# Four neighbouring engines' orders changed together: values before keys, token variance before the score bias, tokens before the second turn, squares summed by rows before gate 0

## The reference

```python
x = x + attention(ln_c(x))     # ln_c: over the 64 channels; 8x8 windows, 4 heads of 16, softmax(q k + bias) v, projection
t = tokens(x)                  # 16384 tokens of 64 channels per image
t = t + moe(ln_t(t))           # router: softmax of 8 logits, top 2, shares renormalised; 8 experts, 64x64 each, with bias
x = back(t)
```

## Time and profile before

| | |
|---|---|
| time, median of 3 runs | 1269.74 us (1269.69 to 1274.37) |
| the profiled execution | 1268.81 us, span 1267.0 us |
| busy: PE, DVE, ACT, POOL | 1192.4, 1053.9, 920.4, 1081.7 us |
| granted clock of PE over the span | 0.983 of full speed |
| the chain that ended last | PE 67%, DVE 10%, POOL 7%, DMA 7%, issue 5%, ACT 5% |

### The profile page before, as it was taken

One profiled execution on the slowest core, in us unless ns is written; L12 is line 12 of the kernel. 1 busy time (PEld: TensorE's weight loads), 2 busy tenths in 40 slices (PEclk: granted clock), 3 DMA queues, 4 the chain that ended last, 5 costly groups with the idle time before them and its releaser, 6 DMA issues.

```text
span 1267.0 us, 47630 instructions
## 1 busy us (share of the span) xinstructions
PE 1192.4 (94%) x19840; PEld 729.4 (58%) x19840; DVE 1053.9 (83%) x2247; ACT 920.4 (73%) x1743; POOL 1081.7 (85%) x925
## 2 busy tenths in 40 slices
PE   4579999999999999999999999999999999999986
PEld 3456666655565666656566666655556565666531
DVE  6458898888888889898888888988888888888874
ACT  6368778867777887877677888777767776777742
POOL 6368999989888999999988899998988888888753
PEclk9599999999999999999999999999999999999998
DMA  7012333322223233322222333332222222222221
GB/s 203 5 38 66 92 94 86 81 61 71 55 60 81 77 90 94 91 59 61 70 55 62 95 88 86 88 87 55 58 65 66 53 65 65 63 56 66 64 70 42
DMA packets 95622, 91.43 MB, mean 72 GB/s; under 512 B 26928, under 2 KB 62384, under 8 KB 95408
## 3 DMA queue, kind: packets, MB, share of 16 engines
q1 hardware_dynamic: 95408, 88.37, 27.6%
HBM read 35.90 MB, written 17.83 MB: 42 GB/s over the span
## 4 chain that ended last, share of the span: by engine, by line
PE 67%; DVE 10%; POOL 7%; DMA 7%; issue 5%; ACT 5%; SPq 0%; DVEq 0%; POOLq 0%; ACTq 0%
PE bank_y L530 16%; PE bank_s L410 8%; PE bank_t L425 8%; PE bank_s L384 6%; PE bank_o L464 4%; PE bank_g L518 4%; DMA r_b<-recip_rows 4%; PE bank_o L438 4%; PE bank_p L454 4%; PE bank_p L518 3%; DVE t_g L992 3%; DMA recip_rows<-r_out 2%; PE bank_t L394 2%; PE bank_y L502 2%; DVE prob L880 2%
## 5 line engine op out<-in xcount | busy, mean ns | idle before, releaser
L1142 POOL TENSOR_TENSOR t_g<-t_t,g_copy 128x512 f32<-128x512 f32 x192 | 245.6, 1292 | 72.0 <-ACT g_copy L712 70.8
L530 PE MATMUL bank_y<-t_g,w_exp 128*64 128x512 f32 x1024 | 268.9, 616 | 6.7 <-DVE t_g L992 4.7
L1120 POOL TENSOR_TENSOR prob<-prob,mx 128x512 f32<-128x512 f32 x256 | 261.8, 1045 | 14.7 <-DVE mx L887 14.5
L675 ACT ACTIVATE prob<-prob 128x512 f32<-128x512 f32 x256 | 159.4, 623 | 128.6 <-POOL prob L1120 128.6
L992 DVE TENSOR_TENSOR t_g<-t_t,bank_p 128x512 f32<-128x512 f32 x256 | 174.2, 680 | 9.2 <-PE bank_p L518 7.3
L880 DVE TENSOR_TENSOR prob<-bank_s,rel 128x1024 f32<-128x1024 f32 x128 | 156.3, 1221 | 28.4 <-PE bank_s L410 23.7
L425 PE MATMUL bank_t<-idn,prob 128*128 128x128 f32 x1024 | 163.6, 283 | 5.5 <-ACT v_bd L670 5.0
L679 ACT ACTIVATE prob_t<-bank_t 128x512 f32<-128x512 f32 x256 | 152.5, 596 | 21.3 <-PE bank_t L425 21.2
L712 ACT ACTIVATE g_copy<-bank_g 128x512 f32<-128x512 f32 x192 | 113.8, 593 | 74.1 <-PE bank_g L518 73.9
L425 PEld LDWEIGHTS bank_t<-idn,prob 128*128 128x128 f32 x1024 | 112.8, 141 | 79.2 <-issue 65.9
L887 DVE TENSOR_REDUCE mx<-prob 128x16 f32<-128x1024 f32 x128 | 155.4, 1214 | 2.2
(11 more groups left out here) (122 smaller groups left out, 2345.1 us busy)
## 6 DMA issues: line engine op xcount, KB each, us to landing
t_t<-t_rout SPq DMA_DIRECT2D x256, 128.0 KB, 2.4
x_in<-in_x SPq DMA_DIRECT2D x68, 256.0 KB, 3.3
r_b<-recip_rows SPq DMA_DIRECT2D x64, 256.0 KB
out_y<-y_out SPq DMA_DIRECT2D x128, 128.0 KB, 2.6
r_in<-sum_b SPq DMA_DIRECT2D x64, 16.0 KB
recip_rows<-r_out SPq DMA_DIRECT2D x64, 16.0 KB, 1.7
t_g<-in_sel SPq DMA_DIRECT2D x1, 512.0 KB, 3.6
rel<-in_relb SPq DMA_DIRECT2D x1, 256.0 KB, 2.9
```

Of the source, the lines that this page charges most:

```text
L530: mm(B_Y[C * a:C * a + C, :], w_exp[:, pair, :], t_g[:, (2 * pair + a) % TG, :], start=False, stop=(pair == MIXES // 2 - 1), skip_group_ch ...
L675: A(prob[:, i], prob[:, i], ACT.Exp).then_inc(p_ready.sem, 1)
L1120: G.tensor_tensor(sc, sc, mx[:, i, :].unsqueeze(2).broadcast_to([P, 2 * HEADS, NTOK]), ALU.subtract).then_inc(s_shifted.sem, 1)
L1142: G.tensor_tensor(t_g[:, u % TG, :], t_t[:, p, u % 2, :], g_copy[:, n, :], ALU.mult).then_inc(tg_pool.sem, 1)
```

## The change

PE's `values` stands before the key and value projection, and `turn_tokens` before the second turn. On ACT the turned gates and the tokens are copied between the two key copies, and the values after the second turn's copy in every slot; in take slots the second block is copied out before the first one is squared. On DVE `token_variance` stands before `bias`, `reciprocals` before `total_squares`, and `sum_squares` before gates 0 and 1. The squares are written as [128 rows, 8], so that ACT writes 32 bytes apart and DVE reads 8 neighbours. No operation is added or removed.

```diff
--- before.py
+++ after.py
@@ -110,7 +110,7 @@
 
         x_in = sb("x_in", [P, RING, 4, W])
-        x_sq = sb("x_sq", [P, 2, 4, H])
+        x_sq = sb("x_sq", [P, H, 2 * 4])
...
@@ -152,7 +152,7 @@
...
-        FIRST_SQ = (x_sq, prob[:, 0:2].rearrange("p i h n k -> p (i h n k)").rearrange("p (m c h) -> p m c h", m=2, c=4))
+        FIRST_SQ = (x_sq, prob[:, 0:2].rearrange("p i h n k -> p (i h n k)").rearrange("p (h x) -> p h x", x=2 * 4))
         B_S = ctx.enter_context(nc.psum_tensor("bank_s", [P, 2, BANK], F32))
         B_T, B_O, B_E, B_P, B_G, B_Y = (
             ctx.enter_context(nc.psum_tensor(f"bank_{n}", [P, BANK], F32)) for n in "toepgy")
@@ -540,19 +540,19 @@
                     prob_sums(j - 1, 1 - p)
                 if attending:
                     turn_probs(j, 0, work)
+                if outputting:
+                    values(j - 1, 1 - p)
                 if projecting:
                     project(j + 1, KEYS_VALUES)
-                if outputting:
-                    values(j - 1, 1 - p)
                 if mixing:
                     residual(j - 3, 1 - p)
                     turn_gates(j - 3)
+                if routing_on:
+                    turn_tokens(j - 2)
                 if work.take:
                     take(work.batch, *work.take, 0, j)
                 elif attending:
                     turn_probs(j, 1, work)
-                if routing_on:
-                    turn_tokens(j - 2)
                 if mixing:
                     expert_biases(j - 3)
                     gates(j - 3, 0)
@@ -625,7 +625,8 @@
                 act.wait_ge(xt_ready.sem, xt_ready.at(n, 2 * r + m + 1))
                 act.wait_ge(sq_sums.sem, sq_sums.at(batch, max(t * 2 + r - (batch == 0), 0)))
                 act.sem_inc(passed, 1)
-                A(dst[:, m], xt[:, bass.ds(plane + (2 * r + m) * 4, 4), :], ACT.Square).then_inc(sq_ready.sem, 1)
+                A(dst[:, :, 4 * m:4 * m + 4].rearrange("p h c -> p c h"), xt[:, bass.ds(plane + (2 * r + m) * 4, 4), :],
+                  ACT.Square).then_inc(sq_ready.sem, 1)
 
             def first_take(batch, t, r):
                 for m in range(2):
@@ -726,19 +727,18 @@
                     copy_result(j - 4)
                 if projecting:
                     copy_k(j + 1, 1 - p, 0)
+                if mixing:
+                    copy_turned_gates(j - 3)
+                if routing_on:
+                    copy_tokens(j - 2)
+                if projecting:
                     copy_k(j + 1, 1 - p, 1)
-                    if not work.take:
-                        copy_v(j + 1)
-                if mixing:
-                    copy_turned_gates(j - 3)
                 if work.take:
                     take(work.batch, *work.take, 0, B_T[:, :])
-                if routing_on:
-                    copy_tokens(j - 2)
-                if projecting and work.take:
+                elif attending:
+                    copy_probs(j, p, 1)
+                if projecting:
                     copy_v(j + 1)
-                if attending and not work.take:
-                    copy_probs(j, p, 1)
                 if routing_on:
                     copy_logits(j - 2)
                 if attending and work.take:
@@ -757,8 +757,8 @@
                 if routing_on:
                     gate_exp(j - 2)
                 if work.take:
+                    take(work.batch, *work.take, 1, B_T[:, :])
                     square_planes(work.batch, *work.take, 0)
-                    take(work.batch, *work.take, 1, B_T[:, :])
                 if mixing:
                     copy_gates(j - 3, 6)
                 if attending:
@@ -817,7 +817,7 @@
                 pair = bass.ds(t * 2 + r, 1)
                 dve.wait_ge(sq_ready.sem, sq_ready.at(n, 2 * r + 2))
                 V.tensor_reduce(sums2[:, :, pair].rearrange("p h o -> p (h o)"),
-                                src[:, :, :, :].rearrange("p m c h -> p h (m c)"), AX.X,
+                                src[:, :, :], AX.X,
                                 ALU.add).then_inc(sq_sums.sem, 1)
 
             def first_sums(batch, t, r):
@@ -995,27 +995,27 @@
                 projecting, attending, outputting, routing_on, mixing = stages(on)
                 if mixing:
                     routing(j - 3, 9, 14)
+                if routing_on:
+                    token_variance(j - 2)
                 if attending:
                     bias(j, 1)
-                if routing_on:
-                    token_variance(j - 2)
                 if mixing:
                     routing(j - 3, 15, 19)
                 if attending:
                     maxima(j, 1)
+                if outputting:
+                    reciprocals(j - 1)
                 if work.step == SQUARES:
                     total_squares(work.batch)
-                if outputting:
-                    reciprocals(j - 1)
                 if work.step == PLANES:
                     total_planes(work.batch)
                 if work.step == SCALES:
                     turn_root(work.batch)
+                if work.sums:
+                    sum_squares(work.batch, *work.sums)
                 if mixing:
                     gate(j - 3, 1 - p, 0)
                     gate(j - 3, 1 - p, 1)
-                if work.sums:
-                    sum_squares(work.batch, *work.sums)
                 if routing_on:
                     routing(j - 2, 1, 8)
                 if mixing:
```

More of the change, by code:

```diff
@@ L728, in slot @@
                     copy_k(j + 1, 1 - p, 0)
-                    copy_k(j + 1, 1 - p, 1)
-                    if not work.take:
-                        copy_v(j + 1)
                 if mixing:
                     copy_turned_gates(j - 3)
+                if routing_on:
+                    copy_tokens(j - 2)
+                if projecting:
+                    copy_k(j + 1, 1 - p, 1)
                 if work.take:
                     take(work.batch, *work.take, 0, B_T[:, :])
-                if routing_on:
-                    copy_tokens(j - 2)
-                if projecting and work.take:
+                elif attending:
+                    copy_probs(j, p, 1)
+                if projecting:
                     copy_v(j + 1)
-                if attending and not work.take:
-                    copy_probs(j, p, 1)
                 if routing_on:
```

## The result

The changed kernel takes **1301.85 us** (median of 4 runs, 1300.98 to 1302.6), the kernel before 1269.97 us beside it; the ratio is 1.0236, 95% interval 1.0219 to 1.0254. The change costs 31.9 us.

A forecast was written before the change was run, and what follows sets the result against it. PE, busy 18.58 of 18.70 us in a steady group, was taken as the bound. Take slots +7.7, plain +10.4, sum -0.7, statistics +3.3 and filling +1 made about +22: 1291 us, eight-in-ten range 1280 to 1303.

The forecast's parts named there:

- The copies behind the later keys: ACT, seven copies from first key to l_t: l_t complete 0.62 us later, PE's gates 3 +0.51 plain, +0.42 take.
- Plain slots: 24 slots without input turns, sums or statistics: 14 grow by 0.51 us and 10 by 0.33, +10.4 in all.
- the late DMA chain: Reciprocals and their two DMAs start 0.3 us later; about ten plain slots, where PE waits behind them, grow by 0.33.
- Values in front cover the bias: PE's projection start: moved to t = 3.66 with 0.3 us of cover from values; without them it would stall 0.7.
- Take slots j%16 = 7 to 10: Among 24 slots that also turn two input blocks: each 0.42 us longer less 0.10 from the shorter reduce, +7.7 in all.
- Statistics slots: Nine slots (j%16 = 12 to 14) doing a statistics step: +0.3, +0.3 and +0.5 us, three times, +3.3.
- the rival of the stalled projection: If ACT's square ends after t = 1.8 in most slots, everything slides 0.3 us in 57 slots: 1308 us, chance 0.07.
- The squares by rows: DVE's reduce 0.77 us shorter in 28 slots; ACT's square 0 to +0.38 longer; start 0 to +3, taken as 0.
- Sum slots: Three slots that only sum squares (j%16 = 11): from 18.71 to 18.46 us, -0.7 in all, turn_logits covering gate 0.

## Why the prediction was right, and where its sizes were off

The forecast of 1291 in 1280 to 1303, slower with 0.86, held: 1301.85, at the upper end. The mechanism was right and the parts together were a third too low; the terms that were mis-sized are named below.

- **The copies behind the later keys (right).** L_t was put at t = 8.35 to 8.72 and came at 8.30 to 8.70. In between, first key 4.83 (forecast 4.83), g_t 5.62 (5.61), t_rout 6.11 (6.11), second key 6.59 (6.61). Gates 3 was to start at 8.87 and does at 8.91. Plain slots 18.48, forecast 18.45. The experiment with l_t ahead of the second probabilities shows the cause: with l_t 0.5 earlier a plain slot falls by 0.49 where nothing else is late. The take slots of the first half of a batch are 19.07, forecast 19.03.
- **Plain slots (+12.6, forecast +10.4).** I let ten of them, with the late DMA chain, grow by 0.33 only, and in sum that was about right: nearly all plain slots are 18.48 now, so most of those that were longer before grew by 0.3 or less (slot 33, at 19.25, by 0.96) and the others by 0.53. The whole excess lies in slots 15, 31 and 47, which grew by 3.2 together; they are told of below.
- **Values in front cover the bias (right, with a bound that failed in some slots).** In plain slots the bias ends at 3.29 and the projection starts at 3.66. Without values in front the change takes 1343.91.
- **Take slots j%16 = 7 to 10 (+0.50, forecast +0.32), the step that failed.** The forecast took the square's end from a plain slot, 1.44, and let POOL gain slack from the longer slots. In these slots the square was late before already, at t = 1.08 in slot 40, which started at 781.83:

```profile
782.91 0.64 ACT L687 ACTIVATE xc<-xc 128x512 f32<-128x512 f32 x1 [0.28 <-POOL xc L1128]
```

POOL's work now stands in a loop with DVE's: centre, square, variance, bias, maxima, shift. The same slot after the change, from 804.91:

```profile
806.10 0.63 ACT L688 ACTIVATE xc<-xc 128x512 f32<-128x512 f32 x1 [0.27 <-POOL xc L1128]
806.76 0.69 DVE L919 TENSOR_REDUCE ln<-xc 128x8 f32<-128x520 f32 x1 [0.77 <-ACT xc L688]
807.37 1.22 DVE L880 TENSOR_TENSOR prob<-bank_s,rel 128x1024 f32<-128x1024 f32 x1
...
808.69 1.10 PE L384 MATMUL bank_s<-xn,w_qkv 64*64 64x128 f32 x32
...
811.31 2.04 POOL L1120 TENSOR_TENSOR prob<-prob,mx 128x512 f32<-128x512 f32 x2 [1.00 <-DVE mx L887]
```

The square starts at t = 1.19 and ends at 1.82, so the bias starts at 2.46 and the projection at 3.78 instead of 3.66; l_t and the slot are 0.15 later than in the first half of a batch (19.21 against 19.07). POOL is busy 17.97 us in this slot, as the stretches show, and idle one more before its shift, so it has hardly any slack left. Before the change DVE began with the bias and only the variance behind it waited for the square, so a late POOL cost the scores nothing.
- **Statistics slots (+4.8, forecast +3.3), and the three plain slots behind them.** This is the rival of the stalled projection, in seven slots (12, 14, 15, 28, 30, 31 and 47) instead of in most; PE stalls there for 0.55 to 0.83 us. In slot 47, from 938.56:

```profile
940.46 0.63 ACT L688 ACTIVATE xc<-xc 128x512 f32<-128x512 f32 x1 [0.27 <-POOL xc L1128]
...
941.73 1.22 DVE L880 TENSOR_TENSOR prob<-bank_s,rel 128x1024 f32<-128x1024 f32 x1
...
943.05 1.10 PE L384 MATMUL bank_s<-xn,w_qkv 64*64 64x128 f32 x32 [0.76 <-issue]
```

The square ends at t = 2.53, past the 1.8 that the rival named, and slots 15, 31 and 47 take 19.68, 19.51 and 19.34 us (18.31, 18.77 and 18.30 before). Slot 45 grew by 0.97 without a stall: there the normalisation waits 1.61 us for the reciprocals' DMAs.
- **The squares by rows.** DVE's reduce was put near 1.21 us and took 1.17. ACT's square was bounded by +0.38 us and took +0.53, so the upper bound of its price was too low. The reduce was also to give 0.10 in each take slot, 2.4 us in all, and no run shows that it did: alone it gave none, and the change with the old squares has the same take slots in the first half of a batch, 19.06, as the change. At the start I took 0 of 0 to +3, because POOL's plane sums queue up there. They did before (first row, twelve without a pause); they no longer do. Timeline of POOL before, then of ACT and POOL after:

```profile
13.61 16.46 POOL L1094 TENSOR_TENSOR plane_sum<-plane_sum,xt 128x512 f32<-128x512 f32 x12 [0.16 <-ACT xt L620]
```

```profile
13.91 2.11 ACT L628 ACTIVATE x_sq<-xt 128x512 f32<-128x512 f32 x2
14.13 2.63 POOL L1094 TENSOR_TENSOR plane_sum<-plane_sum,xt 128x512 f32<-128x512 f32 x2 [0.25 <-ACT xt L620]
...
16.79 2.13 ACT L628 ACTIVATE prob<-xt 128x512 f32<-128x512 f32 x2
17.01 2.62 POOL L1094 TENSOR_TENSOR plane_sum<-plane_sum,xt 128x512 f32<-128x512 f32 x2 [0.25 <-ACT xt L620]
```

A pair of planes now takes ACT 2.88 us (13.91 to 16.79) and POOL 2.63, so ACT sets the pace; with squares of 632 ns it would be 1.06 less. The price was +2.8 us, by the first normalised input. The Trainium skill (SBUF — State Buffer, on cachelines under Door 1) lets each access that crosses to a new 16-byte line pay a penalty. The trace agrees on both sides, 1160 ns against 632 for the write and 1977 against 1172 for the read. The +3 us that the prediction put beside it was the upper end of my own range, and nearer than my 0.
- **Sum slots (+0.4, forecast -0.7).** They take 18.61, 18.72 and 19.27, forecast 18.46. Gates 2 waits for gate 0, which stands behind the reduce, until t = 8.29 to 8.31 and not 8.1, so turn_logits did not quite cover it: gates 3 starts at 9.04 to 9.07. In slot 43 (from 862.58) gates 7 waits as well, for gates behind a normalisation that had waited 1.33 us for the DMAs:

```profile
870.89 0.39 PE L518 MATMUL bank_g<-g_t,gate_sel 128*128 128x512 bf16 x1 [0.70 <-DVE t_g L992]
...
879.55 0.39 PE L518 MATMUL bank_p<-g_t,gate_sel 128*128 128x512 bf16 x1 [0.43 <-DVE t_g L992]
```

- **Not separated.** Take 1 ahead of square 0 and the reciprocals ahead of the totals were not tried alone. The loop in the take slots is read from the trace. With the bias ahead of the variance again the squares of these slots start at t = 0.84 to 0.86, but those slots are 0.35 longer for another reason, so no run took POOL's lateness away by itself.

## What to carry to other kernels

Where engines run fixed orders, find the one result that the bounding engine waits for and lay the work ahead of it end to end with the start-to-start spacings of the trace: that gave the plain slot and the early take slots to 0.04 us here; the slots with a late input it missed by 0.18 and more. Then look at what the first waiting instruction of each other engine newly waits for. An operation that is moved to the front of a queue makes everything behind it hostage to its input, and the slots where that input comes late (statistics, takes) show it before the plain ones do. And a move that costs alone can be the cover for another: test moves by undoing one as well as by doing one.

## What the hardware showed that I had not expected

ACT's activation with 512 float32 results a partition takes 632 ns with neighbours in order and 1160 ns when they are written 32 bytes apart, 1.03 ns more an element. DVE's reduce gained 0.79 ns an element (1977 to 1172 ns for 1024) from reading neighbours instead of 512 bytes apart. So the write on ACT cost more an element than the read on DVE gave back, and over a pair of squares and their reduce the layout takes more engine time than it gives: +1.06 us on ACT, -0.81 us on DVE. The trip of the reciprocals through DRAM is the other one: in slots 33 and 59 of one kernel, whose token variance starts at the same t = 1.85, the wait for it is 1.80 and 0.67 us, and over the plain slots from 15 on it is 0.15 to 1.89 us.
